# A unit's turned maxima: copied once by ScalarE and placed by two transfers, instead of placed by two ScalarE copies

## The chip, the cores and the metric

The kernel runs on one core of one Trainium2 chip. The metric is the device time of one launch in microseconds (us), the median of three runs: 1384.45 us for the kernel before.

## What is computed

Two pre-norm blocks over x of shape 8 x 512 x 256: x += linear attention, x += mixture of experts (top 2 of 8, with a shared expert), x += windowed softmax attention, x += mixture of experts (top 1 of 8). The change lies in the third, which for a batch of 512 tokens, 16 heads of 16 channels and a window of 128 is

```python
q, k, v = proj(Wq, bq), proj(Wk, bk), proj(Wv, bv)      # B, H=16, N=512, d=16
energy = jnp.einsum('bhqd,bhkd->bhqk', q, k)
energy = jnp.where(abs(idx[:, None] - idx[None, :]) > 128, fmin, energy)
att = jax.nn.softmax(energy / jnp.sqrt(jnp.float32(E)), axis=-1)
out = jnp.einsum('bhqk,bhkd->bhqd', att, v)
out = jnp.einsum('bne,fe->bnf', out.transpose(0, 2, 1, 3).reshape(B, N, E), Wp) + bp
```

## The kernel before, in words

The program is written out by hand for five engines, each with its own order of instructions; semaphores tie them. Its stages are a linear-attention and shared-expert stage, the experts of the first mixture (to about 610 us), the windowed attention (about 630 to 1075 us), and the experts of the second mixture.

The windowed attention works through 32 **units** (8 batches x 4 groups of G = 4 heads), `u` = 0 to 31. A unit is spread over steps: `unit(s, first, n)` gives the unit whose work begins `first` steps after step 4u. Four steps later the next unit comes, so several units are in flight. In order:

- **Strips.** Every two units a projection of keys and queries is made (`pe_qk`), split by ScalarE (`act_high`, into `hi`) and VectorE (`dve_low`, into `lo`), and written by SyncE to the DRAM tensor `strips` (`sp_keep`, L2105: three transfers of 256 KB, twice for each pair of units). `sp_place` reads them back into the SBUF tiles of one unit: two transfers into `kz` (keys, L2118, 192 KB each) and one into `qT` (queries, L2120, 384 KB). There are SLOTS = 4 of each. A wait in `sp_place` (L2115) holds it until the strips have landed.
- **Scores, steps 0 to 3.** TensorE multiplies queries by keys (`pe_scores`, L851, 96 rows), and VectorE takes each query's maximum under the mask (`dve_mask`, L1892). After step 3, `dve_maxima` writes the negated maxima as a high and a low part into `max_parts`.
- **Turning the maxima, step 4.** TensorE transposes them into a PSUM bank (`pe_maxima`, L884). ScalarE then copies them into rows 96 to 99 of `qT`, one copy of 4 x 512 for each pair of heads (`act_place_maxima`, L1255). This is the last work of ScalarE in that step but for norms and the shared expert's.
- **Scores again, steps 7 to 10.** TensorE computes the scores a second time, keys by queries over 100 rows, so that the four more rows subtract the maximum (`pe_again`, L873; 16 matmuls per unit, seen in the timeline as pairs). The first of them waits for `maxima_placed`. ScalarE applies the exponential (`act_exp`, L1244, L1246), GpSimd masks (L2037, L2040), and `pe_values` (L898) multiplies by the values.

All of SyncE's transfers, the strips, the placements, the residual (`keep_residual`, L1074) and the normed rows (`keep_normed`, L1069, 512 KB each) of every batch among them, go through one hardware queue in the order of SyncE's program. `fill` makes TensorE wait until the former content of a PSUM bank has been read; for the bank of the maxima that is `maxima_placed` too (`emptied`).

Of the kernel before, what the change touches and what calls it, by code (L numbers as in the profile page):

```python
# [12 lines left out]
F32 = mybir.dt.float32  # L13
F32R = mybir.dt.float32r
# [3 lines left out]
ACT = mybir.ActivationFunctionType  # L18
AX = mybir.AxisListType

P = 128
# [15 lines left out]
G = 4  # L37
# [164 lines left out]
def build(nc, a, out):  # L202
    ctx = ExitStack()
    with ctx:
        def sb(name, shape, dt=F32):
            return ctx.enter_context(nc.sbuf_tensor(name, shape, dt))
# [10 lines left out]
        def over(name, word, shape, dt):  # L217
            return nc.alloc_sbuf_tensor_at(name, shape, dt, offset=arena_at + 4 * word)
# [5 lines left out]

        max_parts = over("max_parts", 8192, [P, TPB, G // 2, 32], F32R)
        work = sb("work", [P, 8192])
        ident = sb("ident", [P, P])
# [39 lines left out]
        def carve(t, at, *shape):  # L267
# [5 lines left out]
            if len(shape) > 1:  # L273
# [125 lines left out]
                "rows_hot", "ones_made", "tokens_found", "tokens_listed"))  # L399
        (pads_zeroed, key_pads_made, pads_made, moe_added, bias_added, v_made, hi_made, lo_made, maxima_placed,  # L400
         mx_made, maxima_made, p_exped, p_masked, less_made, shift_made, oT_made, rec_made, o_made, oT2_act, oT2_dve, proj_added) = (
            sem(n) for n in (
                "pads_zeroed", "key_pads_made", "pads_made", "moe_added", "bias_added", "v_made", "hi_made", "lo_made",
                "maxima_placed", "mx_made", "maxima_made", "p_exped", "p_masked", "less_made", "shift_made", "oT_made", "rec_made",
                "o_made", "oT2_act", "oT2_dve", "proj_added"))
# [10 lines left out]
        def emptied(kind, *k):  # L416
# [47 lines left out]
            if kind == "maxima":  # L464
                return maxima_placed, G // 2 * (k[0] + 1)
            if kind == "values":
# [389 lines left out]
        def pe_again(e, u, j, half):  # L856
# [4 lines left out]
            if j == 0 and half == 0:  # L861
                e.wait_ge(maxima_placed, G // 2 * (u + 1))
            for k in range(2):
# [313 lines left out]
        def act_attention(e):  # L1177
# [3 lines left out]
            for s in range(FIRST_STEP, LAST_STEP):  # L1181
# [23 lines left out]
                for u, _ in unit(s, 4, 1):  # L1205
                    act_place_maxima(e, u)
                for first, norm in ((-14, 2), (37, 3)):
# [40 lines left out]

        def act_place_maxima(e, u):

            if u >= SLOTS:
                e.wait_ge(*done["again", u - SLOTS, TPB - 1, G - 1])
            e.wait_ge(*done["maxima", u])
            for half in range(G // 2):
                e.activation(qT[ROWS_S:ROWS_T, u % SLOTS, half, :], psum[32 * half:32 * half + G, bank_of["maxima", u], :],  # L1255
                             ACT.Copy).then_inc(maxima_placed, 1)

# [849 lines left out]
        def sp_place(e, u):  # L2107
# [9 lines left out]
            for k in range(2):  # L2117
# [4 lines left out]
                        ).then_inc(qk_placed[slot], 16)  # L2122

        def sp_first_weights(e, k):

            if k in LIST_FIRST:
                e.wait_ge(experts_listed, list_of(k) + 1)
            if k == 0:
                e.wait_ge(*done["again", NU - 3, TPB - 1, G - 1])
            if k == 1:  # L2130
                e.wait_ge(*done["values", NU - 2])
            if k >= 2:
                e.wait_ge(*done["up1", k - 2, 1])
            x = e.value_load(blk_expert[0:1, 1, k:k + 1], min_val=0, max_val=NX - 1)
            e.dma_start(w1_now[k % 2].rearrange("p c n -> p (c n)"),
                        a["w1"][bass.ds(x, 1), :, :].rearrange("x p n -> p (x n)")).then_inc(w1_got[k % 2], 16)
# [45 lines left out]
        def _(e):  # L2182
# [4 lines left out]
            for b in range(NBLK0):  # L2187
# [3 lines left out]
                e.dma_start(results[b * P:(b + 1) * P, :], y0[:, b % 3, :]).then_inc(result_kept[b % 3], 16)  # L2191
            for s in range(FIRST_STEP, LAST_STEP):

                for first in (-5, -4):
# [51 lines left out]
```

## Time and profile before

| | |
|---|---|
| median of three runs | 1384.45 us (1383.04 to 1385.96) |
| the profiled execution | 1384.07 us, of which 1382.0 us are the span of the profile |
| busy: TensorE, VectorE, ScalarE, GpSimd | 1329.7, 687.0, 488.3, 446.8 us |
| mean granted TensorE clock | 0.996 of full speed |
| bytes moved by DMA | 254.29 MB, 217.61 MB of them through SyncE's queue |

The profile is of one execution. Busy time is the time in which an engine executes an instruction; a wait is put down to the instruction that released it last. "Landing" of a transfer is when its semaphore has all 16 of its counts. SPq rows in the timeline are the issuing of a transfer by SyncE, not its moving.

### The profile page before, as it was taken

What the parts mean: (1) busy time and instruction counts of PE and PEld (TensorE: products, weight loads), DVE (VectorE), ACT (ScalarE), POOL (GpSimd) and SP (SyncE); (2) the same over time, 40 slices, a digit from 0 to 9 for tenths busy, and PEclk for the clock granted to TensorE, in tenths of its full rate; (3) what the DMA queues carried; (4) which work ended last, traced back from release to release, by engine and by line L of the source; (5) the groups of instructions that cost most, each with busy time, mean ns of one, the idle gap of its engine ahead of it and who ended that gap; (6) DMA issues with size and microseconds to landing.
All of it is one profiled execution on the core that took longest, in us unless ns stands there. A gap on an engine that the chain in (4) does not pass through costs nothing.

```text
span 1382.0 us, 25005 instructions
## 1 busy us (share of the span) xinstructions
PE 1329.7 (96%) x8348; PEld 1029.0 (74%) x8348; DVE 687.0 (50%) x2499; ACT 488.3 (35%) x1046; POOL 446.8 (32%) x541
## 2 busy tenths in 40 slices
PE   7899999999999999999999999999998999999998
PEld 5566556688999999755666666666665799999998
DVE  5655456233333333436888888888888231300000
ACT  2221211122222222122676676666766512111111
POOL 2100000253222222251554454544333534344332
PEclk9999999999999999999999999999999999999999
DMA  9402011067777777233555554655442789999996
GB/s 330 131 31 68 9 37 48 20 225 233 233 236 242 239 235 240 77 111 100 148 140 151 155 151 132 176 137 153 141 121 91 267 301 341 342 338 341 333 348 207
DMA packets 95676, 254.29 MB, mean 184 GB/s; under 512 B 12189, under 2 KB 42271, under 8 KB 85568
## 3 DMA queue, kind: packets, MB, share of 16 engines
q1 hardware_dynamic: 79728, 217.61, 48.5%
q0 software_dynamic: 12096, 32.13, 7.5%
q10 hardware_dynamic: 3728, 2.97, 0.7%
q8 instruction: 69, 1.13, 0.3%
q14 instruction: 55, 0.45, 0.1%
HBM read 201.42 MB, written 52.17 MB: 183 GB/s over the span
## 4 chain that ended last, share of the span: by engine, by line
PE 84%; DVE 8%; issue 4%; ACT 3%; DMA 0%; DVEq 0%; ACTq 0%; POOLq 0%
PE psum L994 10%; PE psum L675 10%; PE psum L1004 10%; PE psum L813 10%; PE psum L796 7%; PE psum L686 6%; PE psum L851 4%; PE psum L898 4%; PE psum L873 4%; PE psum L922 3%; DVE work L1892 3%; PE psum L823 2%; PE psum L768 2%; PE psum L933 2%; PE psum L956 2%
## 5 line engine op out<-in xcount | busy, mean ns | idle before, releaser
L1892 DVE CUSTOM_DVE_ANT_0 work<-psum,mask 128x384 bf16<-128x384 f32 (+1 forms) x512 | 230.0, 484 | 53.5 <-PE psum L851 52.2
L851 PE MATMUL psum<-kz,qT 96*128 96x384 f32 (+1 forms) x512 | 165.3, 391 | 14.2 <-DVE small L1892 12.9
L1971 POOL DMA_INDIRECT work<-normed,token_of x71 | 67.3, 948 | 323.6 <-PE psum L768 196.7
L675 PE MATMUL psum<-arena 128*128 128x512 f32 x320 | 147.5, 599 | 0.0
L994 PEld LDWEIGHTS psum<-arena 128*128 128x128 f32 x1248 | 145.5, 192 | 2.4 <-issue 0.4
L994 PE MATMUL psum<-arena 128*128 128x128 f32 x1248 | 146.1, 275 | 0.0
L813 PEld LDWEIGHTS psum<-work,arena 128*128 128x128 f32 x1136 | 134.9, 191 | 14.8 <-ACT work L1148 11.0
L813 PE MATMUL psum<-work,arena 128*128 128x128 f32 x1136 | 142.1, 278 | 3.6 <-ACT work L1148 2.0
L1244 ACT ACTIVATE arena<-psum 128x384 f32<-128x384 f32 x256 | 112.5, 496 | 85.4 <-PE psum L873 82.7
L1004 PE MATMUL psum<-arena 128*128 128x256 f32 x624 | 141.6, 379 | 0.8 <-issue 0.8
L873 PE MATMUL psum<-qT,kz 100*128 100x384 f32 (+1 forms) x512 | 131.9, 330 | 8.7 <-ACT arena L1244 8.4
L851 PEld LDWEIGHTS psum<-kz,qT 96*128 96x128 f32 x512 | 90.0, 192 | 64.6 <-DVE small L1892 37.5
L1746 DVE TENSOR_TENSOR arena<-psum,arena 128x256 f32<-128x256 f32 x39 | 16.6, 425 | 239.1 <-PE psum L1004 233.3
L1004 PEld LDWEIGHTS psum<-arena 128*128 128x128 f32 x624 | 115.4, 190 | 15.8 <-issue 1.8
L1272 ACT ACTIVATE arena<-psum 128x1024 f32<-128x1024 f32 x39 | 39.9, 1023 | 226.6 <-PE psum L994 203.3
L2037 POOL TENSOR_SCALAR_AFFINE_SELECT arena<-arena 128x512 f32<-128x512 f32 x96 | 62.3, 649 | 176.4 <-ACT arena L1244 152.1
L873 PEld LDWEIGHTS psum<-qT,kz 100*128 100x128 f32 x512 | 87.9, 189 | 30.0 <-ACT arena L1244 28.6
L796 PE MATMUL psum<-arena,work 128*128 (+1 forms) x426 | 103.8, 380 | 0.0
L675 PEld LDWEIGHTS psum<-arena 128*128 128x128 f32 x320 | 60.0, 192 | 57.9 <-issue 56.1
L1246 ACT ACTIVATE arena<-psum 128x512 f32<-128x512 f32 x128 | 75.4, 596 | 54.8 <-PE psum L873 49.0
L686 PE MATMUL psum<-arena,work 128*128 128x256 f32 (+1 forms) x384 | 91.9, 382 | 2.3 <-DVE X L1444 2.3
L686 PEld LDWEIGHTS psum<-arena,work 128*128 128x128 f32 (+1 forms) x384 | 71.3, 189 | 29.1 <-issue 17.6
(243 smaller groups left out, 1983.2 us busy)
## 6 DMA issues: line engine op xcount, KB each, us to landing
arena<-in_w SPq DMA_DIRECT2D x78, 1024.0 KB
arena<-in_wgu SPq DMA_DIRECT2D x71, 704.0 KB, 4.9
strips<-hi SPq DMA_DIRECT2D x64, 256.0 KB
kz<-strips SPq DMA_DIRECT2D x64, 192.0 KB, 3.2
qT<-strips SPq DMA_DIRECT2D x32, 384.0 KB, 4.7
results<-work SPq DMA_DIRECT2D x71, 128.0 KB
strips<-lo SPq DMA_DIRECT2D x32, 256.0 KB
normed<-work SPq DMA_DIRECT2D x14, 512.0 KB, 3.1
```

The costliest lines, as they stand in the source:

```text
L675: m = e.matmul(psum[0:w, bk, :], sgu[:, k, u, c * P:c * P + w], xnT_all[:, b, k, :], start=(k == 0), stop=(k == EC - 1))
L686: m = e.matmul(psum[:, banks[t // 2], (t % 2) * E:(t % 2 + 1) * E], aT_s[0:w, q, t * P:(t + 1) * P], sdn[0:w, c, :], start=(c == 0 and t % ...
L796: m = e.matmul(psum[:, bk, 0:E], aT0[0:IC[c], b % 4, c * P:(c + 1) * P], wd0[0:IC[c], bass.ds(x, 1), c, :], start=(c == 0), stop=(c == DC ...
L813: m = e.matmul(psum[:, b % 2, q * P:(q + 1) * P], wu0[:, b % 4, c, q * P:(q + 1) * P], xsT0[:, b % 2, c * P:(c + 1) * P], start=(c == 0), ...
L851: m = e.matmul(psum[:, bk, at:at + w], qT[0:ROWS_S, slot, half, i * P:(i + 1) * P], kz[slot][0:ROWS_S, hd, lo_key:hi_key], start=True, sto ...
L873: m = e.matmul(psum[:, bk, at:at + w], kz[slot][0:ROWS_T, hd, j * P:(j + 1) * P], qT[0:ROWS_T, slot, half, lo_q:hi_q], start=True, stop=True)
L994: m = e.matmul(psum[:, bk, q * P:(q + 1) * P], w1_now[k % 2][:, c, at:at + P], xsT1[:, k % 2, c * P:(c + 1) * P], start=(c == 0), stop=(c ...
L1004: m = e.matmul(psum[:, bk, 0:E], hT1[:, k % 2, c * P:(c + 1) * P], w2_now[k % 2][:, c, :], start=(c == 0), stop=(c == HC - 1))
L1244: e.activation(pT(u, j)[:, hd, 0:w], psum[:, bk, 0:w], ACT.Exp, scale=1.0 / E ** 0.5).then_inc(p_exped, 1)
L1246: e.activation(pT(u, j)[:, hd - 1:hd + 1, 0:w], psum[:, bk, :].rearrange("p (h n) -> p h n", h=2), ACT.Exp, scale=1.0 / E ** 0.5).then_inc ...
L1892: e.tensor_tensor_reduce(masked[:, n % 2, 0:w], psum[:, bank_of["scores", u, i, hd], at:at + w], mask[:, P - off:P - off + w], 1.0, MASKED ...
L1971: e.indirect_dma_start(out=xs[:, b % 3, :], out_offset=None, in_=normed[l][0:n, :], in_offset=bass.IndirectOffsetOnAxis(ap=token_of[:, l, ...
```

## The change

ScalarE no longer copies the turned maxima twice into `qT`. It copies the 36 rows of the bank once, into `maxima_now`, a tile of its own at word 29440 of the arena, and raises `maxima_turned`. SyncE waits for that and issues two transfers of 4 rows x 2 KB each from `maxima_now` into `qT` (`sp_place_maxima`), at the beginning of its step 4u + 5, ahead of a `sp_place`, a `sp_keep`, a `keep_residual` or a `keep_normed` of the same step. `pe_again` waits for both to land (16 counts each). The wait for the slot's last reader (`done["again", u - SLOTS, ...]`) moves from ScalarE to SyncE; ScalarE waits instead for the landing of the unit before, since `maxima_now` is single. The PSUM bank is free after ScalarE's one copy. The second weight load of the last stage (`sp_first_weights`, k = 1), whose tile covers `maxima_now`, waits for all the placements.

```diff
@@ -223,6 +223,7 @@
         lo = over("lo", 7168, [P, 2, N], F32R)
 
         max_parts = over("max_parts", 8192, [P, TPB, G // 2, 32], F32R)
+        maxima_now = over("maxima_now", 29440, [P, N], F32R)
         work = sb("work", [P, 8192])
         ident = sb("ident", [P, P])
         before = sb("before", [P, P])
@@ -397,11 +398,11 @@
             sem(n) for n in (
                 "picked", "counted", "so_far_made", "placed", "pick_step", "scored", "experts_listed", "list_set", "one_hot_made",
                 "rows_hot", "ones_made", "tokens_found", "tokens_listed"))
-        (pads_zeroed, key_pads_made, pads_made, moe_added, bias_added, v_made, hi_made, lo_made, maxima_placed,
+        (pads_zeroed, key_pads_made, pads_made, moe_added, bias_added, v_made, hi_made, lo_made, maxima_placed, maxima_turned,
          mx_made, maxima_made, p_exped, p_masked, less_made, shift_made, oT_made, rec_made, o_made, oT2_act, oT2_dve, proj_added) = (
             sem(n) for n in (
                 "pads_zeroed", "key_pads_made", "pads_made", "moe_added", "bias_added", "v_made", "hi_made", "lo_made",
-                "maxima_placed", "mx_made", "maxima_made", "p_exped", "p_masked", "less_made", "shift_made", "oT_made", "rec_made",
+                "maxima_placed", "maxima_turned", "mx_made", "maxima_made", "p_exped", "p_masked", "less_made", "shift_made", "oT_made", "rec_made",
                 "o_made", "oT2_act", "oT2_dve", "proj_added"))
 
         aTs_read, pieces_read, count_made, masks_zeroed, token_step = (
@@ -462,7 +463,7 @@
             if kind == "again":
                 return p_exped, exps_before(*k) + 1
             if kind == "maxima":
-                return maxima_placed, G // 2 * (k[0] + 1)
+                return maxima_turned, k[0] + 1
             if kind == "values":
                 return oT_made, k[0] + 1
             if kind == "o":
@@ -859,7 +860,7 @@
             lo_q, hi_q = window(j)
             w = hi_q - lo_q
             if j == 0 and half == 0:
-                e.wait_ge(maxima_placed, G // 2 * (u + 1))
+                e.wait_ge(maxima_placed, 16 * G // 2 * (u + 1))
             for k in range(2):
                 hd = 2 * half + k
                 if w > 2 * P:
@@ -1203,7 +1204,7 @@
                 for b, t in qk_due(s):
                     act_high(e, b, *divmod(t, 2))
                 for u, _ in unit(s, 4, 1):
-                    act_place_maxima(e, u)
+                    act_turn_maxima(e, u)
                 for first, norm in ((-14, 2), (37, 3)):
                     for b, i in batch(s, first, 2):
                         act_norm(e, norm, b, (2 * i, 2 * i + 1))
@@ -1246,14 +1247,15 @@
                     e.activation(pT(u, j)[:, hd - 1:hd + 1, 0:w], psum[:, bk, :].rearrange("p (h n) -> p h n", h=2), ACT.Exp,
                                  scale=1.0 / E ** 0.5).then_inc(p_exped, 1)
 
-        def act_place_maxima(e, u):
-
-            if u >= SLOTS:
-                e.wait_ge(*done["again", u - SLOTS, TPB - 1, G - 1])
+        def act_turn_maxima(e, u):
+
+            if u == 0:
+                for k in range(2):
+                    e.wait_ge(*done["up", B - 1, NC - 1, k])
+            if u > 0:
+                e.wait_ge(maxima_placed, 16 * G // 2 * u)
             e.wait_ge(*done["maxima", u])
-            for half in range(G // 2):
-                e.activation(qT[ROWS_S:ROWS_T, u % SLOTS, half, :], psum[32 * half:32 * half + G, bank_of["maxima", u], :],
-                             ACT.Copy).then_inc(maxima_placed, 1)
+            e.activation(maxima_now[0:32 + G, :], psum[0:32 + G, bank_of["maxima", u], :], ACT.Copy).then_inc(maxima_turned, 1)
 
         def act_high(e, b, c, i):
 
@@ -2121,6 +2123,15 @@
                         queries.rearrange("(q k) s d n -> (k s d) q n", k=2)
                         ).then_inc(qk_placed[slot], 16)
 
+        def sp_place_maxima(e, u):
+
+            if u >= SLOTS:
+                e.wait_ge(*done["again", u - SLOTS, TPB - 1, G - 1])
+            e.wait_ge(maxima_turned, u + 1)
+            for q in range(G // 2):
+                e.dma_start(qT[ROWS_S:ROWS_T, u % SLOTS, q, :].bitcast(F32),
+                            maxima_now[32 * q:32 * q + G, :].bitcast(F32)).then_inc(maxima_placed, 16)
+
         def sp_first_weights(e, k):
 
             if k in LIST_FIRST:
@@ -2129,6 +2140,7 @@
                 e.wait_ge(*done["again", NU - 3, TPB - 1, G - 1])
             if k == 1:
                 e.wait_ge(*done["values", NU - 2])
+                e.wait_ge(maxima_placed, 16 * G // 2 * NU)
             if k >= 2:
                 e.wait_ge(*done["up1", k - 2, 1])
             x = e.value_load(blk_expert[0:1, 1, k:k + 1], min_val=0, max_val=NX - 1)
@@ -2190,6 +2202,8 @@
                 e.wait_ge(y_made[0], b + 1)
                 e.dma_start(results[b * P:(b + 1) * P, :], y0[:, b % 3, :]).then_inc(result_kept[b % 3], 16)
             for s in range(FIRST_STEP, LAST_STEP):
+                for u, _ in unit(s, 5, 1):
+                    sp_place_maxima(e, u)
 
                 for first in (-5, -4):
                     for u, _ in unit(s, first, 1):
```

## Rows read from the trace of the kernel before

**Rows 1.** the page: busy time by engine, PE in slices, chain that ended last
```profile
PE 1329.7 (96%) x8348; PEld 1029.0 (74%) x8348; DVE 687.0 (50%) x2499; ACT 488.3 (35%) x1046; POOL 446.8 (32%) x541
...
PE   7899999999999999999999999999998999999998
...
PE 84%; DVE 8%; issue 4%; ACT 3%; DMA 0%; DVEq 0%; ACTq 0%; POOLq 0%
```

**Rows 2.** windows view: PE, PEld, DVE, ACT, POOL busy, clock, DMA share, GB/s
```profile
820.00:880.00 60.00, 57.13 (x374) 39.94 (x374) 52.11 (x217) 40.11 (x81) 29.88 (x41) 1.00 0.51 144
```

**Rows 3.** the waits of PE, 640 to 1080 us: total us, times, longest
```profile
PE psum L851 <- DVE small L1892: 12.9, 43, 1.4
...
PE psum L873 <- ACT arena L1244: 8.0, 28, 0.6
...
PE psum L907 <- DVE lo L1880: 2.8, 6, 0.5
```

**Rows 4.** the copies of L1255 by their source line: min/median/max ns
```profile
L1255 ACT ACTIVATE qT<-psum x64: 584/586/591, 647.5 to 1071.3; 4x512 fp32r<-4x512 f32 x64
```

**Rows 5.** timeline around unit 17: start us, duration us, instruction
```profile
877.63 1.20 ACT L1255 ACTIVATE qT<-psum 4x512 fp32r<-4x512 f32 x2
...
878.35 0.66 SPq L2105 DMA_DIRECT2D strips<-lo  x1
...
883.48 0.40 PE L873 MATMUL psum<-qT,kz 100*128 100x256 f32 x2
```

**Rows 6.** the timeline around unit 16, same columns
```profile
856.92 0.65 SPq L2105 DMA_DIRECT2D strips<-hi  x1
...
862.64 0.87 SPq L2118 DMA_DIRECT2D kz<-strips  x2
...
863.56 0.43 SPq L2120 DMA_DIRECT2D qT<-strips  x1
...
862.74 1.20 ACT L1255 ACTIVATE qT<-psum 4x512 fp32r<-4x512 f32 x2
...
869.87 0.40 PE L873 MATMUL psum<-qT,kz 100*128 100x256 f32 x2
```

**Rows 7.** the timeline, unit 23: last strip transfer, first matmul of L873
```profile
961.72 0.68 SPq L2105 DMA_DIRECT2D strips<-lo  x1
...
969.50 0.40 PE L873 MATMUL psum<-qT,kz 100*128 100x256 f32 x2
```

**Rows 8.** the timeline, unit 22: transfer into qT, first matmul of L873
```profile
948.90 0.43 SPq L2120 DMA_DIRECT2D qT<-strips  x1
...
953.48 0.40 PE L873 MATMUL psum<-qT,kz 100*128 100x256 f32 x2
```

**Rows 9.** the timeline, unit 0: transfer into qT, first matmul of L873
```profile
650.79 0.43 SPq L2120 DMA_DIRECT2D qT<-strips  x1
...
653.48 0.40 PE L873 MATMUL psum<-qT,kz 100*128 100x256 f32 x2
```

**Rows 10.** DMA issues: count, KB each, median us from issue to landing
```profile
kz<-strips SPq DMA_DIRECT2D x64, 192.0 KB, 3.2
...
arena<-in_swg SPq DMA_DIRECT2D x1, 640.0 KB, 11.3
...
arena<-in_swg SPq DMA_DIRECT2D x1, 64.0 KB, 12.2
```

**Rows 11.** tile qT: what its transfers take from issue to landing
```profile
DMA to landing us min/median/max: 4.3/4.7/6.9
```

**Rows 12.** windows view, columns as in rows 2: strips being written, then read
```profile
858.90:860.90 2.00, 1.95 (x22) 1.14 (x14) 1.89 (x7) 0.67 (x2) 1.64 (x2) 1.00 0.52 181
...
863.50:865.50 2.00, 1.48 (x11) 1.18 (x10) 1.97 (x16) 1.77 (x4) 1.01 (x2) 1.00 0.94 226
```

**Rows 13.** windows view, columns as in rows 2: start of attention, unit 0
```profile
640.00:643.00 3.00, 1.21 (x4) 0.38 (x3) 3.00 (x8) 2.08 (x4) 0.81 (x2) 1.00 0.00 0
...
643.00:650.00 7.00, 6.08 (x20) 5.00 (x21) 4.32 (x23) 1.17 (x2) 2.67 (x2) 0.51 0.42 131
```

## The prediction

> **What bounds the kernel now.** I read the page first: TensorE is busy for 1329.7 of 1382.0 us, and the chain that ended last is 84% TensorE, 8% VectorE and 3% ScalarE [rows 1]. The change touches the windowed attention alone, so the next view is that of a 60 us stretch of it: TensorE 57.1 us busy, VectorE 52.1, ScalarE 40.1, at a clock of 1.00 [rows 2]. TensorE is the bound there, with some 3 us of gaps in 60, VectorE is close behind it, and ScalarE has a third of its time free. The waits of TensorE say what makes the gaps: over the whole stage 12.9 us behind VectorE's maxima, 8.0 us behind ScalarE's exponentials in 28 waits of at most 0.6 us, and 2.8 us behind VectorE's low parts [rows 3]. No wait for the placing of the maxima is among them. So ScalarE's work counts only where it stands in those 8.0 us, and a new wait of TensorE counts in full, less what it takes from later gaps.
>
> **What is removed.** One of the two copies of each unit: 32 x 0.586 = 18.8 us of ScalarE's time [rows 4]. The copy that stays covers more partitions and as many columns, so I keep 0.586 us for it. It is the last work of ScalarE in its step, and the exponentials of the next step come 0.59 us sooner. What TensorE can win is bounded by the 8.0 us, and it is small, since most of those waits are of one exponential on another and stand elsewhere in the steps; reading all gaps of TensorE ahead of L873 between one and two microseconds behind a copy I find 1.5 us of them. I take a gain of 1.5 us, with 0 and 8.0 as its ends. The bank of the maxima comes free 0.59 us earlier, but nobody waits for it now (cost and gain nothing).
>
> **What is added on SyncE and the queue.** Two issues and two landings per unit, and they stand between ScalarE's copy and the first matmul of `pe_again` of the unit. What is the time to be had there? For unit 17 the copies end at 878.83 and the first matmul of L873 of the unit starts at 883.48 (the third pair of the unit before is the last with 384 columns; its last step and the unit's first have 256): 4.65 us [rows 5]. For unit 16 it is 869.87 - 863.94 = 5.9 us [rows 6]. Over the 32 units it is 3.35 us at least, in the last one, and the new copy ends 0.59 us sooner.
>
> A transfer with nothing ahead of it would be in time. The trace has none that is so small; the nearest is the 192 KB of `kz`, 3.2 us to landing [rows 10], under 3.35 + 0.59 = 3.9 us. But most units have something ahead. SyncE's queue is served in order: at the start of the kernel a 64 KB transfer behind 640 KB ones took 12.2 us to land, no less than the 11.3 us of the large one [rows 10]. So the placed maxima land behind whatever SyncE issued before them, and this is the term that decides. There are four kinds of units, by u mod 4.
>
> (a) u mod 4 = 1 and 3: 768 KB of strips are being written, whose third transfer is issued at about the end of the copies. What that takes is seen at unit 16: third issue at 856.92, and SyncE passes its wait for the landed strips and issues `kz` at 862.64, 5.7 us later [rows 6]. For the maxima I add 0.3 us: nothing is the lower end, and 1.5 us, what the 384 KB of `qT` add to `kz` (4.7 against 3.2 us), the upper one [rows 10, 11]; 16 KB are nearer to nothing. Unit 17: 878.35 + 6.0 = 884.35 against 883.48, late by 0.9 us [rows 5]. Unit 23: 961.72 + 6.0 = 967.7 against 969.50, in time by 1.8 us, since that part of the batch has more of TensorE's work in between [rows 7]. The same reading of units 1, 5, 9, 13, 17, 21 and 25 gives 0.9, 0.7, 0.7, 0.9, 0.9, 0.6 and 1.2, together 5.9 us; 29 and 31 have nothing ahead, and 3 to 27 of the other kind are in time.
>
> (b) u mod 4 = 0 and 2: `sp_place` of the unit two later stands ahead in SyncE's program. Its last transfer, 384 KB, takes 4.7 us, 4.3 to 6.9 [rows 11]. Unit 16: 863.56 + 4.7 + 0.3 = 868.6 against 869.87, in time by 1.3 us [rows 6]. Unit 22: 948.90 + 5.0 = 953.9 against 953.48, late by 0.4 us [rows 8], but the stall of unit 21 just before moves TensorE and not the strips that `sp_place` waits for, so that this is gone. The late ones are at the start of the attention, where the strips are behind: unit 0, 650.79 + 5.0 = 655.8 against 653.48, is 2.3 us late [rows 9], and units 2, 4, 6 and 18 are late by 1.7, 1.3, 0.2 and 0.6 after the stall before them is taken off. Together 6.1 us.
>
> The sum is 12.0 us of new waits of TensorE, in 12 units. With nothing for the transfers themselves it is 8.5 us, with 1.5 us each about 25.
>
> **A rule of the skill.** The view of DMA shows how the strips are written: a share of 0.52 while they are, against 0.94 while they are read back [rows 12]. The Trainium skill, in "DMA: Bandwidth & Descriptors", section "Why a DMA increments its semaphore by 16 and not by 1", says that a transfer runs on the largest number of engines up to 16 that divides the outer sizes of both sides, and on the lowest-numbered ones. The write of 8 heads' strips would be on 8, which agrees with the half share, and the placing of 4 rows on 4 of those same 8, so that the free half of the engines does nothing for it. By that rule the terms under (a) stand; were it spread over all 16, they would too, since all 16 counts are waited for.
>
> **What is taken back.** A stall of TensorE lets VectorE and ScalarE catch up, and gaps that would have followed shrink. TensorE has 12.9 + 8.0 + 2.8 = 23.7 us of gaps in 32 units [rows 3], 0.74 us for a unit. In the 12 late units that is 8.9 us, and I take half, 4.4 us (ends: nothing, 8.9). VectorE with 52.1 of 60 us has 1.8 us free in a unit, so a stall of a microsecond doesn't make it the bound.
>
> **Other edits.** The slot's last reader, which SyncE now waits for, is three units back and done. `maxima_now` is single, but the unit before has been placed for over 5 us when ScalarE comes to it. SyncE waits in order for ScalarE's copy, and behind it stand `keep_residual` and `keep_normed` and the next strips; all of these have whole steps to spare, and the strips are written later anyway. The wait ahead of the second weight load of the last stage falls after the last unit's placing. Together nothing; if that cover fails, a scores matmul waits for `kz`.
>
> **Sum.** 12.0 - 4.4 - 1.5 = +6.1 us. The profiled execution took 1384.07 us, 0.4 under the median, so 1384.4 + 6.1 = 1390.5 us.
>
> **The rivals.**
> 1. *The waits hide* (no change). If only the part of TensorE's work in the late units that VectorE sets anyway is moved, or the queue serves the small transfers when the 4 engines that they need are done and not the last one, 8.5 - 8.9 - 1.5 is about -2, up to 12.0 - 8.9 = +3: 1384 us. For it: the lateness is under a microsecond in nine of the twelve. Against: VectorE is idle for 13% of the time.
> 2. *The small transfers are slow*. With 1.5 us and more for their own landing, or `qT` ahead of them at 6.9 us instead of 4.7 [rows 11], the waits are 25 to 30 us in some 20 units; half of 20 x 0.74 taken back and 1.5 gained make +16 to +21: 1403 us. For it: the trace shows no such transfer. Against: 16 KB between landings of 192 and 384 KB.
> 3. *Faster*. ScalarE's copy stands in the path of the exponentials of `pe_again`, and its absence takes away most of the 8.0 us, while the transfers bypass the strips. It decides from where the landing comes under 3.9 us behind the copy, also in units that write strips: 8.0 x 0.6 = 4.8 us less: 1379.5 us. For it: 28 waits on ScalarE, a few just behind the copy. Against it is the 64 KB row [rows 10], and that these waits are on the exponentials' own time.
> 4. *The clock*. Before unit 0, TensorE was busy for 1.21 of 3 us, and the granted clock was 0.51 (of 2.4 GHz, that is its 1.2 GHz level) over the next 7 us [rows 13]. There the stretch lost 3 us or so. If stalls of 1 to 2 us did that in 6 units, 6 x 3 = 18 us more: 1409 us. Against: TensorE is full on both sides of each stall here.
>
> **How the numbers follow.** Forecast 0.43, rival 1 0.26, rival 2 0.12, rival 3 0.14, rival 4 0.05. A measurement of this kernel can tell about 0.2%, 2.8 us, from no change. The forecast's own range goes from 1386.5 (8.5 us of waits, half of it taken back, and 2 gained) to 1397 (15 us of them, and little taken back). The whole range reaches from 1380.5 to 1404, which leaves out a part of rival 3, the upper part of rival 2 and rival 4. Slower by over 0.2%: most of the forecast, 2 and 4, 0.56; within: most of rival 1 and a little of the forecast, 0.27; faster: rival 3 and a little of rival 1, 0.17.
>
> **What would show it.** In the profile of the changed kernel, TensorE should wait for a transfer into `qT` ahead of L873 or its weight load, some 12 times, 12 us in total, in units 0 to 5 with over a microsecond and in the units 9, 13, 17, 21, 25 with under one; the transfers of units behind strips should land 6 us after the third strip's issue, those of units 29 to 31 under 3.2 us after their own. ScalarE's busy time should be 18.8 us less, its copies 32. The gaps behind VectorE should shrink by 4 us. The forecast is wrong if no such waits are there, if the transfers ahead of the maxima don't hold them back, or if waits of 2 us and more stand in the units with u mod 4 = 3.

## The result, and the profile after

The changed kernel takes 1403.87 us (median of five, 1403.03 to 1412.6) against 1385.75 us of five runs before, 18.1 us more by the medians. The ratio, which is estimated from all runs and not from the medians alone, is 1.0149, 95% interval 1.0128 to 1.0170, or 20.6 us. On a second chip it was 1408.96 against 1384.89 us: 1.0176, 1.0159 to 1.0193. The forecast was 1390.5 us, its own range 1386.5 to 1397 us. The profiled execution of the changed kernel took 1412.6 us, with a span of 1410.8.

The page of the changed kernel: busy times, the granted clock in 40 slices, the chain that ended last. These lines answer to [rows 1].

```profile
PE 1342.1 (95%) x8348; PEld 1037.8 (74%) x8348; DVE 692.1 (49%) x2499; ACT 465.1 (33%) x1014; POOL 448.5 (32%) x541
...
PEclk9999999999999999998999999999999999999999
...
PE 81%; DVE 8%; DMA 5%; issue 3%; SPq 2%; ACT 1%; DVEq 0%; POOLq 0%; ACTq 0%
```

There are two things to see. The chain now has 5% of DMA and 2% of SyncE in it, where it had none. And TensorE is busy for 12.4 us more, though it runs the same 8348 matmuls: it works more slowly in places.

The waits of TensorE from 640 to 1110 us (total us, times, longest), which answer to [rows 3]; L874, L852 and L908 are the former L873, L851 and L907:

```profile
PE psum L874 <- DMA qT<-maxima_now: 18.5, 11, 3.0
...
PE psum L852 <- DVE small L1894: 13.6, 43, 1.4
...
PE psum L874 <- ACT arena L1245: 6.1, 24, 0.5
...
PE psum L908 <- DVE lo L1882: 2.8, 6, 0.5
```

The new wait is there, 11 times and 18.5 us. The old waits are nearly what they were: 13.6 against 12.9 us behind VectorE, 6.1 against 8.0 behind ScalarE, 2.8 against 2.8. Next to nothing was taken back.

The tile `maxima_now`: ScalarE's copy is as long as the one it replaces [rows 4], and issuing one 8 KB transfer takes SyncE 0.66 us in the median and up to 1.85, while each of the 192 KB ones into `kz` took half of 0.87 [rows 6].

```profile
L1258 ACT ACTIVATE maxima_now<-psum x32: 591/592/597, 650.8 to 1101.6; 36x512 fp32r<-36x512 f32 x32
...
L2132 SPq DMA_DIRECT2D qT<-maxima_now x64: 584/656/1845, 655.0 to 1102.9; - x64
```

Unit 17 answers to [rows 5]. The third strip transfer is issued at 903.73, the two small ones from 904.45 on, and the matmul that waits for them starts at 910.27, 6.5 us behind the third strip's issue and 1.3 us late:

```profile
903.73 0.61 SPq L2107 DMA_DIRECT2D strips<-lo  x1
...
904.45 2.65 SPq L2132 DMA_DIRECT2D qT<-maxima_now  x2
...
910.27 0.53 PE L874 MATMUL psum<-qT,kz 100*128 100x256 f32 x2 [1.31 <-DMA qT<-maxima_now]
```

Then comes what the prediction gave a chance of one in twenty. The windows view (TensorE, its weight loads, VectorE, ScalarE, GpSimd, clock, DMA share, GB/s) before, on and behind a stretch that begins just after that wait:

```profile
906.00:910.20 4.20, 2.79 (x16) 2.00 (x14) 4.04 (x14) 2.34 (x5) 3.28 (x5) 1.00 0.76 254
...
910.60:914.00 3.40, 3.40 (x26) 1.75 (x28) 2.91 (x13) 1.20 (x2) 1.69 (x3) 0.50 0.60 184
...
914.00:918.00 4.00, 4.00 (x38) 2.82 (x30) 1.88 (x8) 2.17 (x6) 0.15 (x1) 1.00 0.46 147
```

In the 4.2 us ahead of it TensorE was busy for 2.8, the wait included; then the granted clock is 0.50, 1.2 of 2.4 GHz, and TensorE is busy all the time. Its 26 matmuls in 3.4 us stand against 38 in 4.0 us behind. Between the transposes of units 0 and 31 the profile has 35.6 us at the lower clock, against 3.6 in the profile of before.

### The profile page after: what moved, and what is told of

Its sections match the earlier page's. It is cut to its first block, busy times and chain, and to the rows that moved or that the text cites. A ratio compares the mean times of both kernels' runs of the same rounds, so it can differ in the third digit from the quotient of the medians.

```text
span 1410.8 us, 25070 instructions
## 1 busy us (share of the span) xinstructions
PE 1342.1 (95%) x8348; PEld 1037.8 (74%) x8348; DVE 692.1 (49%) x2499; ACT 465.1 (33%) x1014; POOL 448.5 (32%) x541
## 4 chain that ended last, share of the span: by engine, by line
PE 81%; DVE 8%; DMA 5%; issue 3%; SPq 2%; ACT 1%; DVEq 0%; POOLq 0%; ACTq 0%
PE psum L995 10%; PE psum L676 10%; PE psum L1005 10%; PE psum L814 9%; PE psum L797 7%; PE psum L687 6%; PE psum L899 4%; PE psum L874 3%; DMA qT<-maxima_now 3%; PE psum L923 3%; PE psum L852 3%; DVE work L1894 2%; PE psum L824 2%; PE psum L769 2%; PE psum L957 2%
## 5 line engine op out<-in xcount | busy, mean ns | idle before, releaser
L852 PE MATMUL psum<-kz,qT 96*128 96x384 f32 (+1 forms) x512 | 167.0, 394 | 14.2 <-DVE small L1894 13.6
L874 PE MATMUL psum<-qT,kz 100*128 100x384 f32 (+1 forms) x512 | 133.1, 335 | 25.1 <-DMA qT<-maxima_now 18.5
L852 PEld LDWEIGHTS psum<-kz,qT 96*128 96x128 f32 x512 | 91.6, 195 | 65.5 <-DVE small L1894 37.7
L874 PEld LDWEIGHTS psum<-qT,kz 100*128 100x128 f32 x512 | 89.5, 194 | 44.3 <-ACT arena L1245 21.9
```

The source lines that it names most:

```text
L852: m = e.matmul(psum[:, bk, at:at + w], qT[0:ROWS_S, slot, half, i * P:(i + 1) * P], kz[slot][0:ROWS_S, hd, lo_key:hi_key], start=True, sto ...
L874: m = e.matmul(psum[:, bk, at:at + w], kz[slot][0:ROWS_T, hd, j * P:(j + 1) * P], qT[0:ROWS_T, slot, half, lo_q:hi_q], start=True, stop=True)
```

## The experiments

All ratios are to runs of the kernel before on the same chip. Three groups of runs were made, each on another chip, and the kernel before had medians of 1384.89, 1387.37 and 1388.64 us in them, so that ratios are compared and not times. A gain or loss in us is worked out from the ratio, and can differ by 1 or 2 us from the difference of the medians. Two readings of the same runs are used throughout: the waits of TensorE, and the length of the 31 stretches between the transposes of one unit's maxima (L884) and the next unit's.

**The changed kernel once more.**

> The changed kernel once more, for a second profile beside the others. Expected 1403 us, 15 to 19 us of waits of TensorE for the placed maxima in 9 to 12 units, and four to seven falls of the clock within the attention.

Measured 1.0176 (above). Its profile has 12 waits with 16.9 us, and 40.1 us at the lower clock in the attention. So the profile above is no accident: 17 to 18.5 us of waits belong to the change, and 26 to 37 us more at the lower clock than the two profiles of the kernel before have (3.6 and 9.3 us).

**Is it what stands ahead of the transfers?** SyncE places the maxima first in its step 4u + 4.

```diff
-                for u, _ in unit(s, 5, 1):
+                for u, _ in unit(s, 4, 1):
                     sp_place_maxima(e, u)
```

> The changed kernel, with SyncE placing a unit's maxima at its step 4u + 4, ahead of that step's placement of the unit two later and of the strips, instead of behind them. Theory A (what stands ahead in the queue sets the landing): both transfers land about 2.5 us after the first one's issue, as those of units 29 to 31 of the changed kernel do, some 5 us ahead of the first matmul; the 18.5 us of TensorE's waits go to under 2 us, no fall of the clock within the stage beyond the one at its start, time 1382 to 1386 us. Theory B (the small transfers themselves are slow, whatever stands ahead): waits stay at 10 us or more, 1395 to 1404 us.

Measured 1389.04 us, ratio 1.0032 (1.0016 to 1.0047). Its waits, and SyncE's issues around units 21 and 22:

```profile
PE psum L874 <- DMA qT<-maxima_now: 0.3, 1, 0.3
...
PE psum L852 <- DMA qT<-strips: 1.1, 2, 0.6
...
PE psum L852 <- DVE small L1894: 17.9, 47, 1.9
...
940.52 1.24 SPq L2132 DMA_DIRECT2D qT<-maxima_now  x2
...
949.57 3.25 SPq L2107 DMA_DIRECT2D strips<-hi  x1
...
959.73 0.78 SPq L2120 DMA_DIRECT2D kz<-strips  x2
```

The waits for the placed maxima are gone, 0.3 us. So theory A holds for them: a pair of small transfers with nothing ahead is early. But the time is 4 us above that of before, which A didn't expect. The strips now start behind the maxima, in unit 21 some 3.5 us later against the end of the copy than before; with the normed rows between them the next strips are held at their issue, 3.25 us for one of them, and the placement of unit 24 comes at 959.73, 6.5 us behind the issue of unit 22's maxima. The stretches of units 10, 14, 18 and 22 are 0.7, 1.3, 2.1 and 2.2 us longer than in the kernel with one copy (below), and the attention has 15.9 us at the lower clock against 9.2 there. The waits for `qT` themselves are 1.1 us, those behind VectorE 5 us more than before; how the late placement turns into these is read from the timeline, and no run took it apart.

**Is it the order of SyncE's queue?** ScalarE issues the two transfers on its own queue, right behind its copy.

```diff
+            e.wait_ge(maxima_turned, u + 1)
+            for q in range(G // 2):
+                e.dma_start(qT[ROWS_S:ROWS_T, u % SLOTS, q, :].bitcast(F32),
+                            maxima_now[32 * q:32 * q + G, :].bitcast(F32)).then_inc(maxima_placed, 16)
...
```

> The changed kernel, with the two transfers issued by ScalarE on its own queue right behind its copy. ScalarE waits for its copy and issues (2 x 0.65 us) per unit. Theory A (order in SyncE's queue): they are not held by what SyncE issued earlier except for sharing the engines that move data; landing 2.5 to 4 us behind the copy, waits of TensorE on them under 4 us in total, but exponentials come some 0.7 us later than in the changed kernel; 1383 to 1390 us. Theory B (shared data-moving engines hold them, not the queue's order): landing 5 to 6.5 us in units behind strips as before, waits 12 us and more, 1395 to 1404 us.

Measured 1414.25 us, ratio 1.0208 (1.0174 to 1.0242), slower than the changed kernel. The waits of ScalarE and TensorE, then unit 13: two strips' issues, ScalarE's own issue, and the matmul that waits:

```profile
ACT arena L1245 <- issue: 43.2, 23, 2.4
...
PE psum L874 <- ACT arena L1245: 18.7, 43, 1.2
...
PE psum L874 <- DMA qT<-maxima_now: 6.6, 8, 1.2
...
838.30 1.21 SPq L2113 DMA_DIRECT2D strips<-hi  x2
...
839.56 0.64 SPq L2113 DMA_DIRECT2D strips<-lo  x1
...
839.34 2.09 ACTq L1263 DMA_DIRECT2D qT<-maxima_now  x2
...
847.11 0.51 PE L874 MATMUL psum<-qT,kz 100*128 100x256 f32 x2 [1.04 <-DMA qT<-maxima_now]
```

Two things. ScalarE pays for the issuing: 43.2 us of idle time ahead of its exponentials, and TensorE's waits for those exponentials grow from 6.1 to 18.7 us. That is the largest part of the loss here; the waits for the placed maxima are 6.6 us. And on a queue of its own, issued at 839.34, the pair of unit 13 lands at 847.1, 7.8 us later, although SyncE's queue isn't ahead of it. By the counts of its semaphore in the trace, the pair is complete at 847.06, 0.5 us behind the last count of the third strip (846.58); in all odd units from 1 to 27, those behind strips, it is 0.2 to 0.5 us behind it. So it isn't the order of one queue that holds the small transfers behind strips. My 2.5 to 4 us of theory A were wrong for these units. Theory B is right on what holds them, and not in its figures: it had waits of 12 us and more and 1395 to 1404 us. The Trainium skill, "DMA: Bandwidth & Descriptors", section "Queues, rings and completion order", says that the count of a landing is written only after every earlier write of the same data-moving engine, across its queues. The 7.8 us and the 0.5 us behind the strip agree with it; sharing the data-moving engines would look much the same, and no run tells the two apart. It changes no term of the sum.

**What does the removed copy pay?** Only ScalarE's second copy is left out, from unit 4 on.

```diff
-            for half in range(G // 2):
+            for half in range(G // 2 if u < SLOTS else 1):
...
```

> The kernel before, with ScalarE's second copy left out from unit 4 on (the rows of the second pair of heads keep an older unit's maxima, so other numbers are subtracted there); no transfers. It prices the removal by itself. Theory A: 1.5 us gained at most, 1382.5 to 1384.5 us. Rival (ScalarE's copy stands in TensorE's path): 4 us or more gained, under 1381 us.

Measured 1384.19 us, ratio 0.9977 (0.9966 to 0.9987): 3.2 us gained, twice what I took. Where it lies is seen at unit 22. The kernel before, ScalarE's exponentials behind the copies and TensorE's transposes of units 22 and 23:

```profile
948.18 1.90 ACT L1244 ACTIVATE arena<-psum 128x384 f32<-128x384 f32 x4
...
945.73 0.61 PE L884 MATMUL psum<-ident,max_parts 128*36 128x128 f32 x4
...
960.27 0.60 PE L884 MATMUL psum<-ident,max_parts 128*36 128x128 f32 x4
```

The kernel with one copy, the copy, the exponentials, the same transposes:

```profile
947.64 0.59 ACT L1258 ACTIVATE qT<-psum 4x512 fp32r<-4x512 f32 x1
...
949.58 0.87 ACT L1247 ACTIVATE arena<-psum 128x384 f32<-128x384 f32 x2 [0.46 <-PE psum L876]
...
946.41 0.61 PE L887 MATMUL psum<-ident,max_parts 128*36 128x128 f32 x4
...
960.45 0.60 PE L887 MATMUL psum<-ident,max_parts 128*36 128x128 f32 x4
```

From transpose to transpose it is 14.54 us in the one and 14.04 in the other. The same 0.5 us appears in units 6, 10, 14, 18, 22 and 26, and in most of the others almost nothing (up to 0.3 us either way, and more in unit 29, where the clock was at its lower level). These are the units with u mod 4 = 2, where ScalarE also copies the projected rows in that step, so that the exponentials run without a pause behind the copies (four in a row at 948.18) and TensorE waits for them: its second pair of L873 in that step takes 0.83 us, against 0.52 in the kernel with one copy.

**What do the transfers cost if nobody waits?** The kernel before with both copies, and two more transfers per unit at the place of the changed kernel, from the placed rows to unused ones.

```diff
+                at = 32 * (u % SLOTS) + G * q
+                e.dma_start(maxima_now[at:at + G, :].bitcast(F32),
+                            qT[ROWS_S:ROWS_T, u % SLOTS, q, :].bitcast(F32)).then_inc(moved, 16)
```

> The kernel before with both of ScalarE's copies, and in addition two transfers of 4 rows x 2 KB per unit, from the placed rows to unused rows, at the place in SyncE's program that the changed kernel has; TensorE waits for none of them. It prices the transfers and SyncE's waits without TensorE's wait. Theory A (they cost only where TensorE waits): 1384 to 1386 us. Rival (they disturb the strips and placements, or the clock by way of small gaps): 1388 us or more.

Measured 1387.92 us, ratio 1.0002 (0.9989 to 1.0015). The 64 transfers and SyncE's waits for ScalarE cost 2 us at most in that place, and 0.3 us by the ratio. So the loss of some 20 us comes with TensorE's waits.

**Is it the second transfer?** The maxima lie in 8 adjoining rows, and one transfer of 16 KB places a unit (the transposes and ScalarE's copy then have 8 rows and not 36, in lines that are not shown).

```diff
-            for q in range(G // 2):
-                e.dma_start(qT[ROWS_S:ROWS_T, u % SLOTS, q, :].bitcast(F32),
-                            maxima_now[32 * q:32 * q + G, :].bitcast(F32)).then_inc(maxima_placed, 16)
+            e.dma_start(qT[ROWS_S:ROWS_T, u % SLOTS, :, :].bitcast(F32),
+                        maxima_now[0:2 * G, :].bitcast(F32)).then_inc(maxima_placed, 16)
```

> The changed kernel with the maxima of a unit in 8 adjoining rows, so that one transfer of 16 KB places them and not two of 8 KB; same place in SyncE's program. Theory A (order in the queue, plus 0.65 to 1.25 us that SyncE spends on each issue): landing 0.7 to 1.2 us earlier in units behind strips, TensorE's waits 8 to 11 us in place of 17 to 18, fewer falls of the clock: 1393 to 1399 us. Rival (the landing is set by the strips alone, the number of transfers counts for nothing): 1403 to 1409 us.

Measured 1406.7 us, ratio 1.0128 (1.0105 to 1.0152). Its wait of TensorE, and SyncE's issues:

```profile
PE psum L874 <- DMA qT<-maxima_now: 19.3, 13, 2.7
...
L2131 SPq DMA_DIRECT2D qT<-maxima_now x32: 632/677/1252, 653.1 to 1095.0; - x32
```

13 waits with 19.3 us, no less than with two transfers, so that the number of transfers and the 0.65 us of SyncE's second issue are not what makes the kernel late. They aren't in the same units: in the seven units with u mod 4 = 1 the waits are 9.3 us here against 12.7 and 10.6 us in the two profiles with two transfers, and the rest is in units of the other kinds. So the second issue may have a part there, of 1 to 3 us; the transfer still lands 6.1 to 7.5 us behind the third strip's issue. The profile has less time at the lower clock, 16.4 us against 35.6; why waits of the same length were followed by fewer falls here is open.

**Is it the clock?** In nine late units TensorE runs eight extra matmuls ahead of the wait. First the price of these alone, in the kernel before:

```diff
+                if late and k == 0:
+                    for _ in range(FILLERS):
+                        e.matmul(psum[:, bk, 0:w], kz[slot][0:ROWS_S, hd, 0:P], qT[0:ROWS_S, slot, half, 0:w],
+                                 start=True, stop=True)
+                    e.wait_ge(maxima_placed, G // 2 * (u + 1))
```

> The kernel before with the same 8 extra matmuls in units 0, 1, 5, 9, 10, 13, 17, 21 and 25 as in the kernel with fillers, ahead of a wait that is over by then. It prices the fillers. By their columns (256 each, 0.11 to 0.14 us) 8 to 10 us, partly taken back: 1390 to 1394 us. If so, the changed kernel with fillers at 1402.2 us carries 8 to 12 us of waits and falls of the clock, against 24 without them, and the difference is what TensorE's idling costs beyond its length.

Measured ratio 1.0039 (1.0024 to 1.0055), 5.4 us. Then in the changed kernel:

> The changed kernel; in units 0, 1, 5, 9, 10, 13, 17, 21 and 25 TensorE runs 8 more matmuls (scores of 96 rows x 256 columns into the bank that is written next) ahead of its wait for the placed maxima, some 1 to 1.5 us each time; nothing else. Theory A (a good part of the loss is TensorE's clock, which falls to 1.2 GHz behind a wait): the falls behind these units mostly go, though the waits plus fillers are as long as the waits were, and the time falls to 1392 to 1398 us. Rival (the loss is the waits alone): the clock's falls cost nothing to speak of, time 1402 to 1406 us or above.

Measured 1402.17 us, ratio 1.0129 (1.0110 to 1.0148), against 1.0176 of the changed kernel on the same chip: 6.8 us less with 72 more matmuls. Its waits for the placed maxima are 9.1 us, 7.8 less than in the profile of the changed kernel beside it, and the extra matmuls cost 5.4, so waits and work together would give 2.4 us less. The other 4.4 us go with the clock: the mean granted clock of its runs is 0.9905 against 0.983, which is 27 against 49 us at the lower level. By the 0.40 us found below that would be 9 us; the waits are those of one execution each, so the split is rough. By the bare time the rival would fit, whose range begins at 1402 us, and theory A's ends at 1398. But both ranges start from the 1403.9 us of the first runs, and the changed kernel took 1408.96 beside this one. Against that, the fall of 6.8 us with work added is not what waits alone give. It points to the clock and doesn't settle its size; that comes from the fit of the next section.

**A quarter of the units, twice.** Transfers only in units with u mod 4 = 1, behind the strips; copies elsewhere.

```diff
+SENT = [u for u in range(NU) if u % 4 == 1]
...
+            if u not in SENT:
+                for half in range(G // 2):
...
+                return
```

> Only the units with u mod 4 = 1 are placed by transfers, at the place of the changed kernel, behind the strips; all others by copies. As many transfers as in the kernel with those of u mod 4 = 2. Theory A: waits of 1 to 3 us in units 1, 5, 9, 13, 17, 21 and 25, together 10 to 13 us, each microsecond in full, and four to seven windows of 3.4 us at the lower clock at 0.4 us of loss each, 5 to 9 us: 15 to 22 us over the kernel before. Rival (the waits are taken back in the gaps that follow): 5 to 8 us over it.

Measured 1403.66 us, ratio 1.0123 (1.0104 to 1.0143), 17.1 us over the kernel before (15.0 by the medians):

```profile
PE psum L877 <- DMA qT<-maxima_now: 10.0, 7, 1.7
...
PE psum L855 <- DVE small L1904: 13.6, 43, 1.4
```

Seven waits, one in each of the seven units named, with 10.0 us, and 20.4 us at the lower clock. This quarter of the units makes most of the loss. The waits behind VectorE are 13.6 us, as in the changed kernel: again nothing is taken back.

The same with u mod 4 = 2, ahead of the placement:

```diff
+SENT = [u for u in range(NU) if u % 4 == 2]
...
-                for u, _ in unit(s, 5, 1):
-                    sp_place_maxima(e, u)
+                for u, _ in unit(s, 4, 1):
+                    if u in SENT:
+                        sp_place_maxima(e, u)
```

> Only the units with u mod 4 = 2 are placed by transfers, ahead of the placement of the unit two later; all others by ScalarE's two copies as before. In the kernel with one copy these were the units that got shorter (14.55 to 14.03 us between two maxima). Theory A (removal pays 0.5 us there and nowhere else; a transfer costs only where TensorE waits for it, and here nothing is written ahead of it): 3.2 to 4 us under the kernel before, no waits for the transfers. Rival (any unit sent by transfer costs by way of the queue): the same as before or slower.

Measured 1386.23 us against 1388.64, ratio 0.9980 (0.9971 to 0.9990), 2.8 us gained. TensorE's waits behind ScalarE (8.4 us in the kernel before over the same stretch), the transposes of units 22 and 23 (14.04 us apart), SyncE's issues at unit 22:

```profile
PE psum L877 <- ACT arena L1248: 7.5, 28, 0.5
...
948.83 0.61 PE L888 MATMUL psum<-ident,max_parts 128*36 128x128 f32 x4
...
962.87 0.60 PE L888 MATMUL psum<-ident,max_parts 128*36 128x128 f32 x4
...
950.55 1.32 SPq L2142 DMA_DIRECT2D qT<-maxima_now  x2
...
951.99 0.84 SPq L2130 DMA_DIRECT2D kz<-strips  x2
```

No wait for a transfer is left in its view of waits. Each pair is complete 2.6 us behind its first issue. As many transfers as in the kernel above, and the opposite sign. Two things differ: here no strips are being written ahead of the transfers, and the copy that is left out is one that delayed exponentials.

**The gain without a transfer.** In the same units ScalarE makes its two copies behind the first exponentials of the next step.

```diff
+                for u, _ in unit(s, 5, 1):
+                    if u % 4 == 2:
+                        act_place_maxima(e, u)
...
                 for u, _ in unit(s, 4, 1):
-                    act_place_maxima(e, u)
+                    if u % 4 != 2:
+                        act_place_maxima(e, u)
```

> The kernel before with ScalarE's two copies in the units with u mod 4 = 2 moved behind the first exponentials of the next step; nothing else, no transfers. If the 0.5 us per unit of the one-copy kernel are the copies' place ahead of those exponentials, this gives the same gain or more (both copies leave the path, the second half of the exponentials may wait instead): 3 to 5 us under the kernel before. If it is the amount of ScalarE's work, nothing: 0 to 1 us.

Measured 1385.73 us, ratio 0.9981 (0.9971 to 0.9992), 2.6 us gained, a little under the 3 to 5 us that were expected and clear of nothing. As both copies are still made, it was their place and not the amount of ScalarE's work. This and the version with u mod 4 = 2 beat both kernels; they are not told apart from each other.

**The kernel before once more**, for its profile.

> The kernel before once more, for a second profile: falls of the clock at about 42, 269 and 645 us and none in the middle of the attention; 1384 to 1388 us.

Measured 1389.71 us, above the range, and 1.0011 times the other runs of itself (0.9999 to 1.0022), which is what a ratio here can be trusted to. Its windows view from 640 to 1080 us:

```profile
640.00:1080.00 440.00, 415.72 (x2716) 286.81 (x2714) 372.47 (x1567) 281.85 (x563) 198.43 (x276) 0.98 0.49 139
```

The mean clock is 0.98. It has falls of the clock at 41, 269, 645 and 1051 us, and none between 652 and 1051 us. The fall at 269 us is in every profile but the first one of before, so it is no effect of the change, though it is in the difference of the two first profiles.

## Why the prediction was wrong

A sum of the stage can be closed from the traces. I took 11 profiles (before twice, changed twice, and the kernels with one copy, unused transfers, maxima first, one transfer, u mod 4 = 1, u mod 4 = 2 and the later copies), 31 stretches each between transposes, and fitted the length of a stretch by a constant for the unit, the wait for the maxima in it and its time at the lower clock. By that a microsecond of wait costs 1.00 us (standard error 0.03), a microsecond at the lower clock 0.40 us (0.01) beyond that. With these the changed kernel's 27.8 us between the transposes of units 0 and 31 are 18.5 of waits, 32.0 x 0.40 = 12.8 of clock, and about 3.5 of gain. Against the second profile of before, which has 9.3 us at the lower clock by itself, the clock's part is 10.5 us.

The forecast had the right bound and failed in three terms of its sum: the clock, put at 0 and measured at 12.8 us; the waits, 12.0 us and measured at 18.5; and what is taken back, 4.4 us and measured at 0. The gain went the other way, 1.5 us against 3.5.

- **The bound and the place of the cost** were right: TensorE waits ahead of L873 in 11 units, and issues and landings elsewhere cost 2 us at most. That it would be slower was right.
- **The waits under (a)** were forecast at 5.9 us and are 12.7 in the same seven units (3.0, 1.9, 1.6, 2.1, 1.3, 1.6 and 1.1), and 0.8 in unit 3, which I had in time. The step that failed is the landing of 5.7 + 0.3 us behind the third strip's issue. In the seven units the matmul is released 7.1, 7.3, 7.0, 7.3, 6.5, 6.8 and 6.4 us behind it. The counts of the semaphores in the trace divide that: the third strip itself takes 5.9 to 6.7 us, 6.3 in the mean, and the pair is complete 0.3 to 0.9 us behind it, 0.6 in the mean. Both terms were too short: 0.9 us in seven units is 6.3 of the 6.8 us that these waits are longer than forecast. The 5.7 us were read at unit 16, where nothing but strips is in flight. In six of the seven units (not in 25) GpSimd issues a gather of rows (`arena<-results,slot_of`) close to the third strip's issue:

```profile
904.34 0.95 POOL L1999 DMA_INDIRECT arena<-results,slot_of  x1
```

  The trace of before had this already. With such a gather beside it (units 1, 5, 9, 13, 17 and 21) the third strip takes at least 6.1, 6.7, 6.3, 6.1, 5.8 and 6.2 us to its last recorded count, without one 5.3 to 5.8. In the changed kernel it takes 5.7 to 5.9 us in six of the seven units with u mod 4 = 3 up to 27, where there is none. The normed rows can't be the reason in units 1 and 5, which are among the three latest: they aren't issued there. That the gathers lengthen the strips is read from the traces; no run leaves them out. The reading of 5.7 us should have been made in the late units themselves.
- **The waits under (b)** were forecast at 6.1 us and are 4.9, but in other units: 2.0, 2.5 and 0.4 us in units 0, 10 and 22, none in 2, 4, 6 and 18. Unit 10 below: `kz` is issued at 796.90, late, since its strips were, and the pair issued at 798.26 releases the matmul at 804.45.

```profile
796.90 0.78 SPq L2120 DMA_DIRECT2D kz<-strips  x2
...
797.73 0.43 SPq L2122 DMA_DIRECT2D qT<-strips  x1
...
798.26 1.33 SPq L2132 DMA_DIRECT2D qT<-maxima_now  x2
...
804.45 0.52 PE L874 MATMUL psum<-qT,kz 100*128 100x256 f32 x2 [2.53 <-DMA qT<-maxima_now]
```

- **What is taken back**: 4.4 us forecast, nothing measured. A wait costs its full length. TensorE's waits behind VectorE didn't shrink; those behind ScalarE did by 1.9 us, of which the kernel with one copy has 1.5 (6.5 us, from 640 to 1080 us), so that 0.4 us is the most that can have been taken back. The gaps of [rows 3] weren't slack that a stall could use up. My reading is that they come from how the few instructions of one step follow each other and so come again in the next; no run tests that.
- **The gain**: 1.5 us forecast, 3.2 measured (1.8 to 4.7). That is 3.2 us from the kernel with one copy, in time; the 3.5 above is what the fit leaves in the profile. I had read gaps within two microseconds of the copy; the delay runs through four exponentials and shows at the next transposes, 14.54 us apart against 14.04.
- **The clock** was my rival 4, with 1 chance in 20, and it is twice the forecast's whole net: 12.8 us in the profile. I had argued that TensorE was full on both sides of each stall, and discounted the case that [rows 13] show. Rival 2 in part (longer waits) and rival 4 together are what happened; rival 4's 3 us for a fall was too much, the fit gives 1.4 to 2.7. Rival 2's 1403 us is close to the 1403.87 measured by luck: it has 25 to 30 us of waits in some 20 units, half of each gap taken back and no clock, where there are 18.5 us in 11 units, nothing taken back and the clock.

In sum: 12.0 - 4.4 - 1.5 + 0 = 6.1 should have been 18.5 - 0 - 3.5 + 12.8 = 27.8 for the profiled execution. The four runs that weren't profiled took 1403.0 to 1405.4 us, some 9 us less. Their granted clock is 0.985 or 0.986 against 0.982, which is some 10 us less at the lower level, or 4 us by the fit; the other 5 us are open.

## What to carry to other kernels

Where the bound engine is full, price a new wait at its full length and add what its clock may lose behind it; its gaps behind other engines were no reserve here. Read a landing time in the very stretch where it will count, with all that is in flight there. A small transfer wasn't quick here while a large write was in flight, on either queue, so put it where nothing is being written, or keep the copy on an engine with free time and move it behind what others wait for. A copy is worth what it delays at its place, not its busy time: here 0.5 us in every fourth unit, and next to nothing in the others.

## What the runs showed of the hardware that I had not expected

- Issuing an 8 KB transfer from SBUF to SBUF held SyncE for 0.66 us in the median, more than one of 192 KB from DRAM (0.4), and held ScalarE for 0.59 us on its own queue, where it stops the exponentials.
- With nothing ahead (units 29 to 31 of the changed kernel, all pairs with u mod 4 = 2 alone sent) the pair was complete 2.5 to 2.6 us behind its first issue. Behind strips it took 5.1 to 6.6 us on SyncE's queue and 6.5 to 7.7 us on ScalarE's, and ended within 1 us of the third strip.
- With 7 of the 11 waits of the first profile, of 1.1 to 3.0 us in a TensorE that is full otherwise, the granted clock fell to 0.50, during the wait or up to 1.6 us behind it; two waits of 1.6 us and two of under 0.8 us had no fall. A microsecond at that level cost 0.40 us.
